# Gathers of embedding rows over 128 partitions in place of 125 in a graph layer with pre-normalisation

## The chip, the cores and the metric

The kernel runs on one core of one Trainium2 chip. The metric is the device time of the whole program in microseconds (us); lower is better. The median of three runs of the kernel before is 3028.99 us (3013.37 to 3032.68).

## The reference, cut to what matters

There are 12,500 nodes of 256 features and 212,500 edges of 128 features. Each node's row gets a projected sum over its outgoing edges, two gates, and one row out of each of two tables of 512 rows, chosen by its in-degree and its out-degree.

```python
in_deg  = minimum(segment_sum(ones, dst), 511)
out_deg = minimum(segment_sum(ones, src), 511)
sum3d   = segment_sum(edge_attr @ W_sum + b_sum, src)
cent    = sigmoid(centralities @ W_cent + b_cent)
vor     = sigmoid(voronoi_values @ W_vor + b_vor)
h   = relu(layernorm(x))
out = x + (h + z_in[in_deg] + z_out[out_deg] + cent + vor + sum3d)
```

## The kernel before, in words

Nodes are cut into 100 windows of 125 (`NODE_P`): node p*100+w is row p of window w, so a window stands on 125 of the 128 partitions. There are 128 partitions in every SBUF tile, and partitions 125 to 127 of a window's rows are never used for output.

**The sort.** 1,660 tiles of 128 edges and a rest of 20 go through a loop over 416 groups of four (q). VectorE (DVE) makes one-hot matrices, TensorE (PE) ranks the edges by window with them, ScalarE (ACT) reads the positions out, and GpSimd (POOL) writes each tile's 128 rows of 520 bytes to their places in HBM with an indirect DMA (L513; L517 for the last 20). Edges are sorted in four segments. Beside this, in places that the table `side` sets, the same engines load sorted rows back and sum them, count in-degrees into `deg_i` (L708, one column per window, 125 partitions), and work out normalisation and gates into `base`. This takes the time up to about 2716 us. `base` holds 55 windows at a time, so 45 of them ("guests") are stored to the output array and are loaded back in the tail (L464).

**The tail.** From about 2716 us the last segment's pieces are loaded (130 KB each, L408, on SP's queue, 12 slots) and folded into `acc` (L670 on DVE, four matmuls L1001, L697 on DVE). There are 250 pieces; after the first 150 (`ahead`), one window's sums are finished by each further piece. From there the loop makes one step per window, 100 in all, and each step holds: the piece; the fold L697; `out_i`, the out-degrees of two windows in one instruction every second step (L767); the transpose of the sums (L1010 on PE), its copy (L878 on ACT), the bias (L927 on ACT), the product with `w_sum` (L1019 on PE) and three adds on DVE into the window's row of `base`: product (L780), z_in row and z_out row (both L785). Five windows make one store (L886, ACT's queue, 560 KB and 65 KB), and the guests' rows come back from step 28 on, five windows at a time.

**The gathers.** POOL has nothing else in the tail. Its list `z_order` has 200 indirect DMAs, all at L530: 100 of z_in (indices in `deg_i`) and 100 of z_out (indices in `out_i`), each bringing the 125 table rows (1,024 bytes each) of one window into a place. z_out of a window waits for that window's `out_i` (`s_out_deg`). The places are two rings. Ring "others" has 15 places in `edge_ring` and serves all z_out and the first 55 z_in; ring "guests" has 18 places laid over `dst_parts`, `key_f` and `gate_normed`, which the tail no longer needs, and serves the 45 z_in of the guests. A gather into a place waits until the add of the gather that had it before is done (`s_added`). The add (L785) reads partitions 0 to 124 alone. In the step count, `out_i` of a pair of windows is made 5 and 6 steps ahead of the adds that need the rows (`COUNT_LAG` 3, `Z_LAG` 9).

Before the first z_out there are 69 gathers of z_in in the list (51 for the first 55 windows, 18 for guests). The 131 left are 100 of z_out and 31 of z_in.

## Time and profile before

| | us |
|---|---|
| runs, median of 3 | 3028.99 |
| runs, lowest and highest | 3013.37, 3032.68 |
| profiled execution, span | 3079.2 |
| POOL busy in the profiled execution | 1853.9 (60%) |
| DVE busy | 1683.0 (55%) |
| PE busy | 1621.7 (53%) |
| ACT busy | 819.8 (27%) |

The profiled execution is known by its span alone; no time around it was recorded beside it. It is another execution than the three runs. Engines overlap, so their busy times do not add up to the span, and DVE instructions overlap by a part of their length too. "Idle before" is what an engine waited ahead of the instructions of a group, with the instruction or transfer that ended it. A transfer's time in the chain of waits runs from its issue to its landing.

### The profile page before, as it was taken

What the parts mean: (1) busy time and instruction counts of PE and PEld (TensorE: products, weight loads), DVE (VectorE), ACT (ScalarE), POOL (GpSimd) and SP (SyncE); (2) the same over time, 40 slices, a digit from 0 to 9 for tenths busy, and PEclk for the clock granted to TensorE, in tenths of its full rate; (3) what the DMA queues carried; (4) which work ended last, traced back from release to release, by engine and by line L of the source; (5) the groups of instructions that cost most, each with busy time, mean ns of one, the idle gap of its engine ahead of it and who ended that gap; (6) DMA issues with size and microseconds to landing.
All of it is one profiled execution on the core that took longest, in us unless ns stands there. A gap on an engine that the chain in (4) does not pass through costs nothing.

```text
span 3079.2 us, 40112 instructions
## 1 busy us (share of the span) xinstructions
PE 1621.7 (53%) x8689; PEld 1230.9 (40%) x8689; DVE 1683.0 (55%) x5737; ACT 819.8 (27%) x4073; POOL 1853.9 (60%) x1869
## 2 busy tenths in 40 slices
PE   5644555455555432226555554444456665568766
PEld 1223444344333320014444444333355554456655
DVE  7554456666666631346656654333455554468866
ACT  3312222232322332442232322222222222200323
POOL 5556665556565667665555655656655555556676
PEclk7756666666666655557767777767777777789988
DMA  4245433334444443334555555555556666579896
GB/s 122 85 127 151 116 106 107 99 104 122 122 121 121 126 135 106 88 107 137 155 152 164 160 160 161 143 151 148 155 156 181 183 187 178 169 189 231 210 248 187
DMA packets 485070, 451.89 MB, mean 147 GB/s; under 512 B 72407, under 2 KB 444637, under 8 KB 484828
## 3 DMA queue, kind: packets, MB, share of 16 engines
q1 hardware_dynamic: 402782, 300.08, 37.0%
q0 software_dynamic: 78752, 136.44, 14.1%
q10 hardware_dynamic: 3294, 12.80, 1.3%
q8 instruction: 71, 1.16, 0.2%
q14 instruction: 171, 1.40, 0.2%
HBM read 319.28 MB, written 129.59 MB: 146 GB/s over the span
## 4 chain that ended last, share of the span: by engine, by line
another core or an unknown queue 34%; DVE 19%; PE 17%; issue 15%; ACT 7%; DMA 3%; SPq 2%; POOL 2%; DVEq 1%; ACTq 0%; POOLq 0%
PE bank L1001 8%; ACT junk L864 6%; DVE hot_dh L605 3%; DVE hot_n L670 3%; DVE acc L697 2%; DVE hot_dl L605 2%; PE bank L949 2%; POOL sorted L513 2%; DMA edge_ring<-in_L_gnn_z_out_dram,out_i 2%; SPq L408 2%; DVE gate_normed L736 2%; PE bank L984 1%; PE bank L1026 1%; DVE hot_t L605 1%
## 5 line engine op out<-in xcount | busy, mean ns | idle before, releaser
L513 POOL DMA_INDIRECT sorted<-edge_ring,pos_i x1660 | 1605.8, 967 | 1103.1 <-DVE pos_i L799 633.4
L1001 PE MATMUL bank<-piece_ring,hot_n 128*125 128x129 f32 x4920 | 885.4, 336 | 260.0 <-DVE hot_n L670 209.0
L864 ACT ACTIVATE junk<-bank,mark_col 128x100 bf16<-128x100 f32 x1664 | 550.4, 343 | 1748.6 <-remote 1221.3
L1001 PEld LDWEIGHTS bank<-piece_ring,hot_n 128*125 128x125 f32 x4920 | 823.2, 241 | 367.0 <-DVE hot_n L670 248.7
L697 DVE TENSOR_TENSOR acc<-bank,acc 125x129 f32 x1230 | 352.8, 287 | 698.6 <-remote 523.9
L984 PE MATMUL bank<-hot_w,after_b 128*128 128x400 bf16 x416 | 189.3, 455 | 806.1 <-ACT junk L864 560.7
L670 DVE SCALAR_TENSOR_TENSOR hot_n<-bank,wkey,piece_ring 128x250 f32<-128x250 f32 x1230 | 579.9, 472 | 11.8 <-issue 5.2
L984 PEld LDWEIGHTS bank<-hot_w,after_b 128*128 128x128 bf16 x416 | 49.5, 119 | 866.8 <-ACT junk L864 594.3
L864 ACT ACTIVATION_READ_ACCUMULATOR junk<-bank,mark_col 128x1 f32 x1664 | 338.1, 203 | 12.3 <-issue 12.3
L605 DVE TENSOR_TENSOR hot_dl<-dst_parts,bank 128x400 bf16<-128x400 bf16 x416 | 148.0, 356 | 337.1 <-remote 305.5
L1026 PE MATMUL bank<-hot_dl,hot_dh 128*125 128x100 bf16 x1661 | 207.2, 276 | 237.4 <-DVE hot_dh L605 197.6
L1026 PEld LDWEIGHTS bank<-hot_dl,hot_dh 128*125 128x125 bf16 x1661 | 182.1, 188 | 268.7 <-DVE hot_dh L605 213.8
L949 PE MATMUL bank<-hot_t,ones_b 128*128 128x400 bf16 x416 | 157.1, 430 | 84.5 <-DVE hot_t L605 52.9
L985 PE MATMUL bank<-hot_w,unmark_b 128*128 128x400 bf16 x416 | 191.1, 459 | 0.0
L978 PE MATMUL bank<-hot_w,before_b 128*128 128x400 bf16 x416 | 189.4, 455 | 0.2 <-DVE hot_w L605 0.2
L605 DVE TENSOR_TENSOR hot_dh<-dst_parts,bank 128x500 bf16<-128x500 bf16 x416 | 170.7, 410 | 0.0
L605 DVE TENSOR_TENSOR hot_t<-src_w,bank 128x400 bf16<-128x400 bf16 x416 | 136.7, 358 | 36.3 <-PE bank L949 22.4
L530 POOL DMA_INDIRECT edge_ring<-in_L_gnn_z_out_dram,out_i x100 | 123.6, 1236 | 53.6 <-DVE out_i L767 18.4
L605 DVE TENSOR_TENSOR hot_w<-src_w,bank 128x400 bf16<-128x400 bf16 x416 | 148.2, 357 | 0.1
L799 DVE CAST pos_i<-pos_f 128x4 int32<-128x4 f32 x416 | 75.0, 180 | 115.7 <-remote 57.5
L949 PEld LDWEIGHTS bank<-hot_t,ones_b 128*128 128x128 bf16 x416 | 47.6, 114 | 176.4 <-DVE hot_t L605 93.2
L927 ACT ACTIVATE bank<-rows_b,acc 125x256 f32<-125x256 f32 x100 | 47.8, 478 | 241.4 <-DVE acc L697 159.2
(109 smaller groups left out, 1183.2 us busy)
## 6 DMA issues: line engine op xcount, KB each, us to landing
piece_ring<-sorted SPq DMA_DIRECT2D x1230, 130.0 KB
edge_ring<-in_edge_attr_dram SPq DMA_DIRECT2D x332, 320.0 KB
sorted<-edge_ring,pos_i POOLq DMA_INDIRECT x1660
base<-in_x_dram SPq DMA_DIRECT2D x20, 560.0 KB
out_dram<-base ACTq DMA_DIRECT2D x19, 560.0 KB
out_dram<-base SPq DMA_DIRECT2D x9, 560.0 KB
base<-out_dram SPq DMA_DIRECT2D x9, 560.0 KB
edge_ring<-in_L_gnn_z_out_dram,out_i POOLq DMA_INDIRECT x100
```

What stands on the lines that cost most here:

```text
L513: g.indirect_dma_start(rows, bass.IndirectOffsetOnAxis(index, 0), edge_ring[:, slot, at, :], None).then_inc(s_scatter[slot], 16)
L530: g.indirect_dma_start(places[n % len(places)][0:NODE_P, :], None, table[:, :], bass.IndirectOffsetOnAxis(index[0:NODE_P, w:w + 1], 0)).th ...
L605: return v.tensor_tensor(to, part.unsqueeze(2).to_broadcast([P, 2, n, 2]), iota_pair[:, 0:n, :].unsqueeze(1).to_broadcast([P, 2, n, 2]), A ...
L670: v.scalar_tensor_tensor(out=hot_n[:, n % HOT_SLOTS, 0:G, :], in0=iota_ps.unsqueeze(1).to_broadcast([P, G, LOC]), scalar=wkey[:, s % 2, c: ...
L697: v.tensor_tensor(to, piece_sums(s, c), to, ALU.add).then_inc(s_summed, 1)
L864: last = a.activation(junk[:, t, :], part[:, t // 2, :, t % 2], ACT.Relu, bias=mark_col[:, :], accum_out=pos_f[:, q % 4, t:t + 1])
L949: return t_.matmul(ps_total[:, 0:SW * QUAD], ones_b[:, :], hot.rearrange("p g w t -> p (g w t)"), start=(h == quad0[s]), stop=(h == quad0[ ...
L978: t_.matmul(ps_rank, before_b[:, :], hot, start=False, stop=True, skip_group_check=True).then_inc(s_rank, 1)
L984: t_.matmul(ps_rank, after_b[:, :], hot, start=False, stop=False, skip_group_check=True)
L985: t_.matmul(ps_rank, unmark_b[:, :], hot, start=False, stop=True, skip_group_check=True).then_inc(s_based, 1)
L1001: last = t_.matmul(to, hot_n[:, n % HOT_SLOTS, k, :], piece_ring[:, n % PIECE_SLOTS, k, 0:SUM], start=(k == 0), stop=(k == ROW_GROUPS[s] - 1))
L1026: last = t_.matmul(ps_in_count, hot_dh[:, b, t // 2, :, t % 2], hot_dl[:, b, t // 2, :, t % 2], start=(h == 0 and t == 0), stop=(h == NQ - ...
```

## The change

The indirect DMA of L530 covers all 128 partitions of its place and of its index column. `deg_i` and `out_i` are written on partitions 0 to 124 only, so both are cleared whole at the start; partitions 125 to 127 then hold index 0 and get row 0 of the table, which no instruction reads.

```diff
@@ gpsimd: gathers
-                g.indirect_dma_start(places[n % len(places)][0:NODE_P, :], None, table[:, :],
-                                     bass.IndirectOffsetOnAxis(index[0:NODE_P, w:w + 1], 0)
+                g.indirect_dma_start(places[n % len(places)][:, :], None, table[:, :],
+                                     bass.IndirectOffsetOnAxis(index[:, w:w + 1], 0)
                                      ).then_inc(landed[n % len(places)], 16)
@@ vector: clears at the start
             v.memset(mark_col[:, :], -MARK)
             v.memset(zero_col[:, :], 0.0)
+            v.memset(deg_i[:, :], 0)
+            v.memset(out_i[:, :], 0)
             v.memset(ones_b[:, :], 1.0).then_inc(s_cleared, 1)
```

On POOL, in the tail, the order of the gathers before (the names are the place's tile, the table in HBM and the index table):

```order
21 L530 DMA edge_ring<-in_L_gnn_z_out_dram,out_i 125x256 x2
22 L530 DMA edge_ring<-in_L_gnn_z_in_dram,deg_i 125x256
23 L530 DMA edge_ring<-in_L_gnn_z_out_dram,out_i 125x256 x3
24 L530 DMA edge_ring<-in_L_gnn_z_in_dram,deg_i 125x256
25 L530 DMA edge_ring<-in_L_gnn_z_out_dram,out_i 125x256 x3
```

The same place of the changed kernel:

```order
21 L530 DMA edge_ring<-in_L_gnn_z_out_dram,out_i 128x256 x2
22 L530 DMA edge_ring<-in_L_gnn_z_in_dram,deg_i 128x256
23 L530 DMA edge_ring<-in_L_gnn_z_out_dram,out_i 128x256 x3
24 L530 DMA edge_ring<-in_L_gnn_z_in_dram,deg_i 128x256
25 L530 DMA edge_ring<-in_L_gnn_z_out_dram,out_i 128x256 x3
```

No gather moves in the list; each has three more partitions. On DVE, at the very start, the changed kernel has:

```order
9 L558 MEMSET mark_col 128x1
10 L559 MEMSET zero_col 128x1
11 L560 MEMSET deg_i 128x100
12 L561 MEMSET out_i 128x100
13 L562 MEMSET ones_b 128x128
14 L563 MEMSET ones_f 128x1
```

Rows 11 and 12 are new, ahead of the clear of `ones_b`, which raises `s_cleared`; all later lines of the program stand two lines further down.

## Rows read from the trace of the kernel before

**Rows 1.** The page: span, and busy time by engine.
```profile
span 3079.2 us, 40112 instructions
PE 1621.7 (53%) x8689; PEld 1230.9 (40%) x8689; DVE 1683.0 (55%) x5737; ACT 819.8 (27%) x4073; POOL 1853.9 (60%) x1869
```

**Rows 2.** Chain of waits, 2860 to 3046 us: start, length, what.
```profile
by line: DMA edge_ring<-in_L_gnn_z_out_dram,out_i 31.8%; issue 19.3%; PE bank L1019 14.5%; PE bank L1001 10.5%; PE bank L1010 6.7%; DVE base L785 2.3%; DVE base L780 2.1%; DVE hot_n L670 2.1%; DVE acc L697 1.8%; DVEq L385 1.6%; POOL edge_ri
...
2903.20 9.83 DMA edge_ring<-in_L_gnn_z_out_dram,out_i
...
2948.12 13.03 DMA edge_ring<-in_L_gnn_z_out_dram,out_i
```

**Rows 3.** Windows of the tail: stretch, busy time (instructions), clock, DMA share, GB/s.
```profile
core 0: us, PE busy (x) PEld busy (x) DVE busy (x) ACT busy (x) POOL busy (x), PEclk, DMA share, GB/s
2860.00:2890.00 30.00, 20.81 (x119) 17.46 (x119) 20.97 (x69) 9.81 (x28) 23.74 (x20) 0.94 0.64 168
2890.00:2918.00 28.00, 21.89 (x129) 17.75 (x128) 22.96 (x78) 10.57 (x31) 18.34 (x16) 1.00 1.00 255
2918.00:3046.00 128.00, 91.74 (x440) 74.70 (x438) 86.38 (x281) 38.33 (x109) 101.96 (x83) 0.85 0.96 232
3046.00:3062.00 16.00, 12.82 (x77) 10.78 (x78) 13.48 (x46) 6.66 (x19) 11.42 (x10) 1.00 0.58 160
```

**Rows 4.** Windows for L780 alone, one instruction per step.
```profile
2890.00:2918.00 28.00, 6.47 (x16) 1.00 1.00 255
2918.00:3046.00 128.00, 23.26 (x55) 0.85 0.96 232
3046.00:3062.00 16.00, 3.84 (x9) 1.00 0.58 160
```

**Rows 5.** Groups of POOL, 2918 to 3046 us: busy, mean ns, idle before.
```profile
L530 POOL DMA_INDIRECT edge_ring<-in_L_gnn_z_out_dram,out_i x56 | 69.6, 1244 | 18.3 <-issue 11.9 <-DVE base L785 3.9 <-DVE out_i L767 1.3
L530 POOL DMA_INDIRECT dst_parts<-in_L_gnn_z_in_dram,deg_i x12 | 14.6, 1216 | 3.7 <-issue 3.4 <-DVE base L780 0.3
L530 POOL DMA_INDIRECT key_f<-in_L_gnn_z_in_dram,deg_i x9 | 11.0, 1225 | 2.8 <-issue 1.8 <-DVE base L785 0.6 <-DVE base L780 0.3
L530 POOL DMA_INDIRECT gate_normed<-in_L_gnn_z_in_dram,deg_i x6 | 7.5, 1248 | 1.8 <-issue 1.5 <-DVE base L785 0.3
```

**Rows 6.** Group of DVE, 2918 to 3046 us, that adds rows from edge_ring.
```profile
L785 DVE TENSOR_TENSOR base<-edge_ring,base 125x256 f32<-125x256 f32 x55 | 23.2, 422 | 34.7 <-DMA edge_ring<-in_L_gnn_z_out_dram,out_i 18.2 <-issue 14.9 <-DVE base L780 0.8
```

**Rows 7.** POOL in order of time: start, length, [idle before].
```profile
2860.45 1.20 POOL L530 DMA_INDIRECT edge_ring<-in_L_gnn_z_out_dram,out_i  x1 [14.93 <-DVE out_i L767]
2861.96 1.20 POOL L530 DMA_INDIRECT edge_ring<-in_L_gnn_z_out_dram,out_i  x1 [0.31 <-DVE out_i L767]
...
2913.99 1.20 POOL L530 DMA_INDIRECT edge_ring<-in_L_gnn_z_out_dram,out_i  x1 [2.51 <-DVE base L780]
...
3046.99 1.44 POOL L530 DMA_INDIRECT edge_ring<-in_L_gnn_z_out_dram,out_i  x1 [0.94 <-DVE out_i L767]
```

**Rows 8.** Groups of POOL over the whole span: scatters and the gathers of z_out.
```profile
L513 POOL DMA_INDIRECT sorted<-edge_ring,pos_i x1660 | 1605.8, 967 | 1103.1 <-DVE pos_i L799 633.4 <-issue 469.1 <-ACT edge_ring L871 0.6
L530 POOL DMA_INDIRECT edge_ring<-in_L_gnn_z_out_dram,out_i x100 | 123.6, 1236 | 53.6 <-DVE out_i L767 18.4 <-issue 17.7 <-DVE base L780 10.6
...
L517 POOL DMA_INDIRECT sorted<-edge_last,pos_i x1 | 0.9, 897 | 0.3 <-issue 0.3
```

**Rows 9.** DMA queues, 2200 to 2300 us: packets, MB, share of 16 engines.
```profile
q0 software_dynamic: 1857, 3.87, 10.9%
```

**Rows 10.** POOL's instructions in two windows: 2200 to 2300, 2716 to 2860.
```profile
2200.00:2300.00 100.00, 56.05 (x60) 0.74 0.54 151
2716.00:2860.00 144.00, 83.16 (x69) 0.93 0.89 226
```

**Rows 11.** DMA queues, 2716 to 2860 us.
```profile
q0 software_dynamic: 8832, 8.91, 24.2%
```

**Rows 12.** Start of the program on DVE, in order of time.
```profile
1.36 0.17 DVE L560 MEMSET ones_b<- 128x128 bf16 x1
...
5.93 0.21 DVE L583 TENSOR_SCALAR base<-base 128x100 f32<-128x100 int32 x1 [1.43 <-DMA base<-in_src_dram]
```

## The prediction

> **What bounds the kernel now.** I read the page's busy times first [rows 1]: no engine is over 60%, so shares say nothing and the stage that the change touches has to be read by itself. All 200 gathers lie after 2716 us. The first 69 are z_in rows of windows that wait for nothing else, gathered while DVE works on pieces. So the chain of waits comes next, for 2860 to 3046 us [rows 2]. Its largest part, 31.8%, is "DMA edge_ring<-z_out": from the issue of a gather to its landing, 9.83 us at 2903 and 13.03 us at 2948. That looks like a slow transfer. The windows view and POOL's own groups tell it otherwise for most of the stretch.
>
> In 2918 to 3046 us POOL has 83 gathers [rows 3, 5]. They are busy for 69.6+14.6+11.0+7.5 = 102.7 us and idle for 18.3+3.7+2.8+1.8 = 26.6 us, together 129 of 128 us, and 26.6/83 = 0.32 us is the gap that stands even between two gathers issued back to back (0.31 at 2861.96 [rows 7]). POOL never rests there: one gather takes 1.24+0.32 = 1.55 us, and a step that needs 83/55 = 1.51 gathers [rows 4] takes 128/55 = 2.33 us. The reader should see that POOL's issue sets this pace. DVE shows the other side: before the adds from `edge_ring` it is idle for 34.7 us in 55 steps, 18.2 of it ended by a z_out landing, and 14.9 by "issue", which is a release whose source the profile doesn't show [rows 6]. Other waits of DVE in the stretch are small against this.
>
> Two stretches beside it are different. In 2890 to 2918 us there are 16 gathers for 16 steps, and POOL waits (2.51 us at 2913.99 [rows 7]), because it has caught up with the indices that DVE makes. A step takes 28/16 = 1.75 us. In 3046 to 3062 us it is 16/9 = 1.78 us, with POOL waiting again. This is the pace of the loop through DVE, PE and ACT when gathers don't hold it. From 3062 on, the last steps run through PE alone.
>
> **The change, part by part.**
>
> (a) *POOL's time per gather.* 125 rows take 1.236 us [rows 8]. No row shows a gather of 128 partitions, so I bound it by neighbours: a scatter of 128 partitions takes 0.967 us and one of 20 takes 0.897 us [rows 8], so the number of rows costs almost nothing (0.07 us for 108 rows, 0.6 ns each) and 105 rows more than 20 don't explain 1.236. Something else does. The queue rows name it: 60 scatters made 1857 packets, about 31 each [rows 9, 10], but 69 gathers made 8832, exactly 128 each [rows 10, 11]. A scatter's 67 KB in some 31 packets are 16 of 4.2 KB (eight rows of 520 bytes) and as many small ones, so each of 16 engines moves eight rows and signals. At that size a gather's 125 KB would need 32 and 16, 48 in all. One split that does give 128 is that 125 = 5 x 25 goes to five engines only, with 25 rows each in seven packets plus a signal, and that the other eleven queues get as many small fillers: 8 x 16. 128 rows = 16 x 8 can be split as the scatter's are. I take the scatter's figure, 0.97 us, as the same count of partitions in the same kind of instruction; the other end is no gain at all, 1.24 us, if a gather is simply dearer than a scatter. Saving 0.27 us per gather.
>
> The Trainium skill, "DMA: Bandwidth & Descriptors", section "Why a DMA increments its semaphore by 16 and not by 1", says that the engines used are the largest number up to 16 that divides the slowest dimension. By that rule 125 gives 5 and 128 gives 16; the 128 packets agree. The same section has an exception that speaks against the change: software-generated direct copies may use all 16 engines with an uneven share. By the exception the old gather would already be spread and the sum would be zero; 128 packets in place of some 48 do not fit it.
>
> (b) *The stretch 2918 to 3046 us.* POOL's need falls from 128 to 83 x (0.97+0.32) = 107 us, 21 us less. What is late next? The loop's own pace, 55 x 1.77 = 97 us, would allow 31. DMA is the nearer limit: 232 GB/s x 128 us = 29.7 MB, and at 255 GB/s, the most that these windows show [rows 3], that is 116 us, which allows 12 us only. DMA share is 0.96 already. But the fillers go (80 packets of each gather), and one engine need no longer move 25 rows while eleven move none, so I expect more than 255. Ends: 0 (POOL doesn't get faster) and 31. I take 17, between DMA's 12 and POOL's 21.
>
> (c) *The stretch 2890 to 2918 us.* POOL waits for indices, DVE hardly for rows. A shorter landing helps a few adds. Ends 0 and 4; I take 2.
>
> (d) *2860 to 2890 us.* POOL is back to back here (20 gathers, 30 us) but is ahead: the first z_out add comes some five steps after its index. Ends 0 and 20 x 0.27 = 5; I take 1.
>
> (e) *The first 69 gathers and the end.* In 2716 to 2860 us POOL is busy for 83 of 144 us [rows 10] and waits for places that DVE frees; faster issue is hidden behind DVE's pieces. After 3062 us only five gathers are left. Both 0.
>
> (f) *Bytes.* 200 x 3 x 1,024 bytes = 0.6 MB more; the 83 gathers of (b) have 0.25 MB, 1 us at 255 GB/s, charged there. All three spare partitions read row 0.
>
> (g) *The two clears.* They stand ahead of `s_cleared` on DVE. `ones_b`, 128 columns, took 0.17 us [rows 12], so two of 100 columns cost at most 0.34 us. The signal releases ACT's small index load, for which DVE then waits 1.43 us, so this is on the path, in full: 0.3 us. No other engine's work is queued behind them.
>
> Sum: 17+2+1-1-0.3 = 19 us, rounded. It is made against the profiled span of 3079.2 us, which gives 3060. That execution is 50 us longer than the median of the runs; none of the terms comes from that difference, so I take the 19 us off the median: 3028.99 - 19 = 3010 us.
>
> **The rivals.**
>
> *R1: no gain, because a gather costs POOL what it costs.* For it: every gather in the trace takes at least 1.2 us whatever its table and place, and its rows are twice as long as a scatter's. Against it: row count alone costs 0.6 ns, and the packets show a different split. The landing might still shorten, but POOL would hold the pace: 0 to 3 us, 3028 us.
>
> *R2: the full release.* If DMA isn't a limit once its load is even, the tail falls to the loop's pace: 31 in (b), 4 in (c), 3 in (d), less 1: 37 us, 2992 us. For it: DVE's 34.7 us of waiting before these adds is about that size. Against it: POOL's 107 us would still stand over 97, unless its mean falls under the scatter's.
>
> *R3: contention.* A gather now has to be served by all 16 engines, each of which also has 5 KB packets of stores and guests' rows, and lands with the slowest of them. The place is steps 28 to 73, where DMA share is about 1. If each landing there took 13.03 us where it takes 9.83 now, a loop over the five steps between index and add gets 3.2 us longer. 45 steps have nine such loops: +29 us, and with POOL's gain lost in waiting, 3059 us with the 1 us for bytes. It decides as soon as index to landing is over five steps of 2.33 us = 11.7 us. Against it: an engine serves two packets of a gather in place of seven, so it should be done sooner.
>
> *R4: the change doesn't do what it says*: the cleared partitions make no difference in the split. Same time as R1, and counted there.
>
> **How the numbers follow.** The forecast (POOL at about 0.97 us, 10 to 30 us gained) has 0.66, R1 0.14, R2 0.14, R3 0.06. The predicted time is the forecast's, 3010 us. Gains of 30 and 10 us are 2999 and 3019. The range takes in R1 and a good part of the way to R2: 2991 to 3031. A measurement of this kernel tells about 1%, 30 us, from no change. Faster by over that is R2 and the edge of the forecast, 0.19. Slower by over that is half of R3 and a little for what I haven't thought of, 0.04. The rest is 0.77.
>
> **What would show it.** POOL's gathers at L530 near 0.97 us in place of 1.236, and 48 packets each in place of 128; in the middle of the tail, POOL no longer back to back; the 34.7 us before the adds from `edge_ring` down to some 10; steps of 2.0 us in place of 2.33; landings in the chain of 5 us or less in place of 9 to 13. DMA share near 1 with over 255 GB/s would say that DMA is the next limit. Gathers that still take 1.2 us make (a) wrong and with it nearly all. Gathers of 0.97 us with a tail that isn't shorter make (b) wrong.

## The result, and the profile of the changed kernel

The changed kernel took **3061.68 us** (median of 4 runs, 3052.53 to 3066.99) against 3027.90 us (4 runs, 3013.37 to 3032.68) of the kernel before beside it: ratio **1.0113**, 95% interval 1.0084 to 1.0143, some 34 us slower. The forecast was 3010 us in a range of 2991 to 3031. The experiments below add a second finding that turns the first one round: on three other chips the same change makes the kernel 1.7% *faster*.

The page of the changed kernel, for [rows 1] the span and busy times, then the row of the DMA queue that carries scatters and gathers, and the chain that ended last by engine:

```profile
span 3065.2 us, 40114 instructions
PE 1626.2 (53%) x8689; PEld 1235.1 (40%) x8689; DVE 1676.7 (55%) x5739; ACT 819.8 (27%) x4073; POOL 1806.1 (59%) x1869
...
q0 software_dynamic: 62752, 136.83, 13.4%
...
another core or an unknown queue 37%; DVE 21%; PE 16%; issue 13%; ACT 7%; POOL 3%; DVEq 2%; DMA 1%; SPq 0%; ACTq 0%; POOLq 0%
```

POOL's busy time fell by 48 us. The queue carried 78752 packets in a profile of the kernel before (its row is shown with e13 below) and carries 62752 now: 16000 fewer, 80 for each of 200 gathers, so 128 have become 48.

The profiled execution of the kernel before (3079.2 us) is no good yardstick for the total: its last scatter was issued at 2712 us, against 2668 to 2674 us in e1 to e4 and the changed kernel. It looks like the runs on chip B below (3073 us), but its chip is not on record. From here on stages are compared, and the yardstick is the kernel before run again (e1_same, span 3026.5 us).

POOL's gathers and DVE's adds of the changed kernel. First two groups of POOL over the whole span, which answer to [rows 8], then three groups of DVE in 2902 to 3030 us, which answer to [rows 6]; columns as there (busy, mean ns, idle before and what ended it):

```profile
L530 POOL DMA_INDIRECT edge_ring<-in_L_gnn_z_out_dram,out_i x100 | 104.0, 1040 | 101.5 <-DVE out_i L769 73.6 <-issue 17.8 <-DVE base L782 5.5
L530 POOL DMA_INDIRECT edge_ring<-in_L_gnn_z_in_dram,deg_i x55 | 52.0, 945 | 68.7 <-DVE base L787 60.3 <-issue 8.5
```

```profile
L787 DVE TENSOR_TENSOR base<-edge_ring,base 125x256 f32<-125x256 f32 x53 | 22.1, 418 | 0.3 <-DMA edge_ring<-in_L_gnn_z_out_dram,out_i 0.3
L782 DVE TENSOR_TENSOR base<-bank,base 125x256 f32<-125x256 f32 x53 | 22.1, 417 | 12.2 <-remote 8.3 <-PE bank L1021 1.9 <-issue 1.6
L699 DVE TENSOR_TENSOR acc<-bank,acc 125x129 f32 x53 | 15.0, 283 | 32.4 <-remote 20.1 <-PE bank L1003 11.6 <-issue 0.6
```

What the prediction wanted of the gathers came true in the main. They are shorter: z_in rows take 945 ns in place of 1202, z_out rows 1040 on the mean in place of 1236 (their median is 949, the longest took 1355). And the add from `edge_ring`, which stood idle for 34.7 us in such a stretch [rows 6], now waits for 0.3 us. POOL is no longer back to back: it waits 73.6 us for the indices that DVE makes, 18.4 before [rows 8]. But the time didn't go away. It turned up at DVE's adds of matmul results, at L699 and L782, as waits for "remote". That word stands where a wait ended and the profile shows no engine or transfer that was still at work on what was waited for. L699 waits for no other engine than TensorE; L782 waits for TensorE's product and, from window 55 on, for the guests' rows too.

The windows of the tail, which answer to [rows 3] (stretch, busy time and instructions, clock, DMA share, GB/s):

```profile
2874.00:2902.00 28.00, 23.04 (x142) 19.44 (x141) 25.12 (x86) 12.43 (x36) 17.67 (x17) 1.00 0.91 282
2902.00:3030.00 128.00, 85.52 (x422) 73.61 (x422) 83.11 (x273) 36.82 (x104) 79.95 (x81) 0.81 0.76 227
```

In the 128 us in the middle every engine did less than before, POOL 80.0 us in place of 102.0 (its gathers are shorter), PE 85.5 in place of 91.7, DVE 83.1 in place of 86.4, and the DMA share fell from 0.96 to 0.76. No engine is full and no queue is. What holds the loop has no row of its own.

It shows best ahead of that, where 21 gathers follow each other without a gap and nothing else changes. First what was waited for (total, times, longest) in 2786 to 2820 us, then the windows around it:

```profile
DVE acc L699 <- remote: 21.3, 5, 6.0
```

```profile
2776.00:2786.00 10.00, 8.66 (x57) 7.06 (x56) 9.81 (x34) 0.00 (x0) 4.11 (x5) 1.00 0.85 255
2786.00:2796.00 10.00, 5.23 (x33) 4.18 (x34) 5.50 (x17) 0.00 (x0) 7.56 (x9) 0.88 0.68 205
2796.00:2806.00 10.00, 2.22 (x8) 1.61 (x8) 1.12 (x4) 0.00 (x0) 7.57 (x9) 0.50 0.46 132
2806.00:2816.00 10.00, 2.44 (x8) 1.85 (x8) 1.25 (x4) 0.00 (x0) 5.41 (x6) 0.50 0.40 118
2816.00:2826.00 10.00, 8.04 (x47) 7.33 (x48) 9.02 (x30) 0.00 (x0) 0.00 (x0) 0.76 0.53 151
```

DVE's column (the third) goes 9.81, 5.50, 1.12, 1.25, 9.02: for 20 us it does next to nothing, PE with it, and both are back within 4 us of the end of POOL's last gather there (2812.9 us). In order of time, two rows of PE and three of DVE (start, length, idle before):

```profile
2790.76 0.71 PE L1003 MATMUL bank<-piece_ring,hot_n 128*125 128x129 f32 x4 [0.68 <-issue]
...
2795.77 1.22 PE L1003 MATMUL bank<-piece_ring,hot_n 128*125 128x129 f32 x4 [2.53 <-DVE hot_n L672]
```

```profile
2790.24 0.47 DVE L672 SCALAR_TENSOR_TENSOR hot_n<-bank,wkey,piece_ring 128x250 f32<-128x250 f32 x1
...
2799.95 0.29 DVE L699 TENSOR_TENSOR acc<-bank,acc 125x129 f32 x1 [4.24 <-remote]
...
2805.55 0.29 DVE L699 TENSOR_TENSOR acc<-bank,acc 125x129 f32 x1 [4.92 <-remote]
```

In this segment DVE's add L699 runs two pieces behind L672 (`FOLD_LAG` 2). The add at 2799.95 us therefore belongs to the piece that L672 prepared at 2790.24, and whose four matmuls ended at 2790.76 + 0.71 = 2791.47 us. The add came 8.5 us later, and for the last 4.2 us of them DVE was idle. The piece of the matmuls that ended at 2796.99 was added at 2812.55, 15.6 us later.

What is late is the signal. An engine tells the others that an instruction is done by raising a semaphore, and the trace holds the times at which semaphores were raised. TensorE's semaphore for the piece that ended at 2791.47 was raised at 2799.82, and DVE and SP's loads, which both wait for it, went on at that moment. The next two came at 2805.42 and 2812.42, 12.2 and 15.4 us after their matmuls; the three after them came together, at 2816.67 to 2816.79, when the gathers had stopped. DVE's own signals came within 0.1 us in the same stretch. The clock isn't the trigger: it was full when the first of these matmuls ran (0.71 us for four) and fell to 0.50 only when PE stood idle between them. The ends of matmuls are modelled in the profile, but the same is seen below with an instruction of ACT.

The same had been in the profile of the kernel before, in the sort, where POOL issues scatters without a gap; I hadn't read it. Its chain by engine, and ACT's group that waits for PE's counts:

```profile
another core or an unknown queue 34%; DVE 19%; PE 17%; issue 15%; ACT 7%; DMA 3%; SPq 2%; POOL 2%; DVEq 1%; ACTq 0%; POOLq 0%
...
L864 ACT ACTIVATE junk<-bank,mark_col 128x100 bf16<-128x100 f32 x1664 | 550.4, 343 | 1748.6 <-remote 1221.3
```

In the sort it is not TensorE alone. One of its stretches, with ACT's last read of a group, DVE's conversion and PE's matmul that wait for it:

```profile
1216.36 0.20 ACT L864 ACTIVATION_READ_ACCUMULATOR junk<-bank,mark_col 128x1 f32 x1 [1.61 <-issue]
```

```profile
1224.10 0.39 DVE L799 CAST pos_i<-pos_f 128x4 int32<-128x4 f32 x1 [10.90 <-remote]
```

```profile
1224.12 0.52 PE L984 MATMUL bank<-hot_w,after_b 128*128 128x400 bf16 x1 [10.73 <-remote]
```

ACT was done at 1216.56 us, its semaphore was raised at 1224.07, 7.5 us later, and PE and DVE started together. So signals of ACT come late too.

**The theory of the pace**, which the experiments test: when POOL issues indirect DMAs of 128 rows back to back, one each 1.25 us, the signals that TensorE's results are there (below: late results) come late by microseconds. Gathers of 125 rows came each 1.50 us and did it much less. Rivals: the clears or the moved start; the 128 rows themselves (their spread over all 16 engines) whatever the pace.

### The profile page after: what moved, and what is told of

The parts are those of the page before. It is cut to its first block, busy times and chain, and to the rows that moved or that the text cites. A ratio compares the mean times of both kernels' runs of the same rounds, so it can differ in the third digit from the quotient of the medians.

```text
span 3065.2 us, 40114 instructions
## 1 busy us (share of the span) xinstructions
PE 1626.2 (53%) x8689; PEld 1235.1 (40%) x8689; DVE 1676.7 (55%) x5739; ACT 819.8 (27%) x4073; POOL 1806.1 (59%) x1869
## 3 DMA queue, kind: packets, MB, share of 16 engines
q0 software_dynamic: 62752, 136.83, 13.4%
## 4 chain that ended last, share of the span: by engine, by line
another core or an unknown queue 37%; DVE 21%; PE 16%; issue 13%; ACT 7%; POOL 3%; DVEq 2%; DMA 1%; SPq 0%; ACTq 0%; POOLq 0%
PE bank L1003 7%; ACT junk L866 6%; POOL sorted L513 3%; DVE hot_n L672 3%; DVE acc L699 3%; DVE hot_dh L607 3%; PE bank L951 3%; DVE hot_dl L607 2%; DVE gate_normed L738 2%; PE bank L1021 2%; DVE hot_t L607 1%; PE bank L986 1%; DVE hot_w L607 1%; PE bank L980 1%
## 5 line engine op out<-in xcount | busy, mean ns | idle before, releaser
L699 DVE TENSOR_TENSOR acc<-bank,acc 125x129 f32 x1230 | 348.3, 283 | 731.0 <-remote 530.3
L672 DVE SCALAR_TENSOR_TENSOR hot_n<-bank,wkey,piece_ring 128x250 f32<-128x250 f32 x1230 | 575.2, 468 | 5.9 <-issue 4.3
L607 DVE TENSOR_TENSOR hot_dl<-dst_parts,bank 128x400 bf16<-128x400 bf16 x416 | 146.0, 351 | 325.7 <-remote 281.1
L530 POOL DMA_INDIRECT edge_ring<-in_L_gnn_z_out_dram,out_i x100 | 104.0, 1040 | 101.5 <-DVE out_i L769 73.6
L1021 PE MATMUL bank<-w_sb,hot_t 128*125 128x256 f32 x200 | 78.9, 481 | 64.4 <-ACT hot_t L880 41.8
```

The lines of the kernel that those rows point to most:

```text
L607: return v.tensor_tensor(to, part.unsqueeze(2).to_broadcast([P, 2, n, 2]), iota_pair[:, 0:n, :].unsqueeze(1).to_broadcast([P, 2, n, 2]), A ...
L672: v.scalar_tensor_tensor(out=hot_n[:, n % HOT_SLOTS, 0:G, :], in0=iota_ps.unsqueeze(1).to_broadcast([P, G, LOC]), scalar=wkey[:, s % 2, c: ...
L699: v.tensor_tensor(to, piece_sums(s, c), to, ALU.add).then_inc(s_summed, 1)
L1021: t_.matmul(ps_y[n % 2][0:NODE_P, 0:D], sumT[:, n % 2, :], w_sb[:, :], start=False, stop=True, skip_group_check=True).then_inc(s_y, 1)
```

## The experiments

They fell on five chips. By the time of the kernel before these are of two kinds, and this turned out to matter more than any edit:

| runs | chip | kernel before, us |
|---|---|---|
| e1 to e4 | A | 3028.03 |
| e5 to e8 | B | 3073.45 |
| e9 to e12 | C | 2479.83 |
| e13 to e16 | D | 2479.36 |
| e17, e18 | E | 2482.66 |

All ratios are against the kernel before on the same chip. ("Theory A" and "theory B" in the expectations of e1 to e4 have nothing to do with the chips' letters.) In the diffs the declarations of semaphores and counters are left out. The stages of each profile, from the starts of POOL's first gather and first z_out gather, and the span:

| profile (chip) | first gather, us | to first z_out gather | from there to the end | both |
|---|---|---|---|---|
| before (not on record) | 2716.7 | 143.8 | 218.8 | 362.5 |
| e1, before (A) | 2674.2 | 137.9 | 214.4 | 352.3 |
| e2, before with the clears (A) | 2673.1 | 135.0 | 210.4 | 345.5 |
| changed kernel (its chip is like A) | 2676.7 | 169.4 | 219.1 | 388.5 |
| e4, changed (A) | 2670.9 | 166.7 | 224.8 | 391.5 |
| e3, changed, clears on POOL (A) | 2674.4 | 163.2 | 224.2 | 387.4 |
| e8, sort paced, gathers of 125 rows (B) | 2602.8 | 146.0 | 219.7 | 365.7 |
| e5, each 1.49 us (B) | 2706.6 | 149.1 | 213.7 | 362.9 |
| e6, each 1.65 us (B) | 2714.9 | 129.1 | 228.4 | 357.5 |
| e7, 1.25 us but spread (B) | 2705.2 | 149.1 | 228.3 | 377.4 |
| e13, before (D) | 2136.7 | 129.8 | 211.0 | 340.8 |
| e14, changed (D) | 2140.2 | 114.3 | 181.6 | 296.0 |
| e15, each 1.49 us (D) | 2140.8 | 114.5 | 209.4 | 323.9 |
| e16, first 69 of 125 rows (D) | 2138.5 | 128.0 | 187.1 | 315.1 |
| e17, first 69 each 1.49 us (E) | 2142.0 | 113.9 | 183.2 | 297.1 |
| e18, changed (E) | 2140.6 | 114.0 | 183.7 | 297.7 |

**e1_same** is the kernel before, unchanged.

> The kernel before, unchanged, for a second profile of it: what two profiles of one kernel differ by, and what two timings of it differ by. Both theories expect a ratio of 1.000 within 0.4%. If its profile puts the first gather within 10 us of 2716.7 us and the time from there to the end within 5 us of 362.5 us, the two profiles of before and after can be compared stage by stage; if it is off by 30 us or more, the sort's length is chance from one execution to the next and the stages have to be compared over several profiles.

Measured: 3027.15 us, 1.0002 (0.9982 to 1.0023). Its first gather came 42 us earlier than in the profile of the kernel before, so by the expectation stages have to be compared over several profiles; three with gathers of 125 rows on this kind of chip (before, e1, e2) differ by 9 us in the first stage and by 8 in the second. At the place in the program where the changed kernel's DVE falls to 1.12 us in 10, its windows are

```profile
2773.00:2783.00 10.00, 8.02 (x51) 6.24 (x49) 8.70 (x29) 0.00 (x0) 7.86 (x8) 1.00 1.08 249
2783.00:2793.00 10.00, 7.75 (x39) 6.14 (x40) 7.55 (x25) 0.00 (x0) 7.93 (x7) 0.86 0.99 228
```

DVE goes on at 8.70 and 7.55 us in 10, with POOL as busy as there but with 7 or 8 gathers in place of 9.

**e2_clears** has the two clears alone:

```diff
+            v.memset(deg_i[:, :], 0)
+            v.memset(out_i[:, :], 0)
```

> The kernel before with the two clears alone, gathers of 125 rows. Theory A (the loss lies in the tail, where a gather now needs all 16 DMA engines): ratio 1.000, since the start is 0.5 us later at most. Theory B (the loss comes from the start: the first keys are later by 0.5 us, or the program is placed otherwise, and the sort runs longer): ratio 1.011, with the tail as before.

Measured: 3025.98 us, 1.0009 (0.9986 to 1.0033). The clears, and what they delay at the start, cost nothing that can be measured.

**e3_gather** has the gathers of 128 rows, with the clears made by POOL in place of DVE:

```diff
+            g.memset(deg_i[:, :], 0)
+            g.memset(out_i[:, :], 0)
-            v.memset(deg_i[:, :], 0)
-            v.memset(out_i[:, :], 0)
```

> Gathers of 128 rows, with the two clears on POOL ahead of its last iota in place of DVE. Theory A: ratio 1.011, first gather to end 20 to 30 us longer than before, and first keys at 5.9 us as before. Theory B: ratio 1.000 or less.

Measured: 3064.98 us, 1.0135 (1.0093 to 1.0178), as theory A had it. With the clears off DVE the cost stays, and e2 had the clears without it: the cost is in the gathers.

**e4_again** is the changed kernel once more.

> The changed kernel again, for a second profile: ratio 1.011 by both theories. Theory A expects first gather to end near 388.5 us again and POOL's gathers at 0.95 us; by theory B that length varies and the sort is longer than before's on the mean.

Measured: 3055.09 us, 1.0097 (1.0066 to 1.0128). The cost is there again.

**e5_pace** keeps the 128 rows and slows POOL down: an iota of 128 columns behind each gather, for which POOL waits, so that gathers come each 1.49 us.

```diff
+                g.iota(start_of[:, 0, 0:128], pattern=[[1, 128]], base=0, channel_multiplier=0,
+                       allow_small_or_imprecise_dtypes=True).then_inc(s_pad, 1)
+                pads += 1
+                pool.wait_ge(s_pad, pads)
```

> The changed kernel with a small iota of POOL (128 columns) behind each gather, and a wait for it, so that gathers come every 1.5 to 1.6 us as before the change, not every 1.25 us. Theory P (what costs time is the pace: while POOL issues DMAs of 128 rows back to back, PE's results come late): first gather to first fold back from 34 us to some 22 us, first z_in add to first z_out gather back from 131 us to some 114 us, ratio to before 1.000 or slightly less. Theory Q (what costs time is that each gather uses all 16 DMA engines, at any pace): both stretches stay at some 34 and 131 us, ratio 1.011 or more.

Measured on chip B: 3076.93 us, 1.0006 (0.9988 to 1.0025). **e6_wider** has an iota of 320 columns there, one gather each 1.65 us.

> As the last, with an iota of 320 columns: a gather every 1.9 us or so. Theory P: no late PE results in the two early stretches (22 and 114 us or less), but the steps from 28 to 75 need 1.5 gathers each and now wait for POOL: 2.9 us per step, some 25 us more, ratio 1.008. Theory Q: 34 and 131 us and the slower steps as well, ratio 1.02.

Measured: 3068.26 us, 0.9978 (0.9957 to 0.9999). **e7_spread** isn't paced (1.25 us), but mixes the guests into the first 69 gathers and ties each of them to a fold, so that no run of them is long (the new order of the list is left out here):

```diff
+                if at < len(early) and 2 * at > 14:
+                    pool.wait_ge(s_summed, piece0[NS - 1] + 2 * at - 14)
```

> The changed kernel with the first 69 gathers spread out: the 18 of guests are mixed into the 51 others, and gather n (from the eighth on) waits until 2n-14 pieces of the last segment are folded, so that no run of back-to-back gathers is left before the first z_out. The pace of the later gathers is untouched. Theory P: the two early stretches fall to 22 and 114 us or less, the steps 28 to 75 stay 9 us longer than before, ratio 1.002. Theory Q: each of the 69 gathers costs what it cost, stretches together still 29 us longer than before, ratio 1.011.

Measured: 3086.42 us, 1.0042 (1.0025 to 1.0059). Of the totals, e5's fits theory P (1.000) and not Q (1.011), e7's lies between P's 1.002 and Q's 1.011 and nearer to P, and e6's is below both (1.008 and 1.02). P's 136 us for the first stage (22 + 114) were missed: e5 and e7 took 149.1. They had been taken from chip A; e8 below, on chip B with gathers of 125 rows, took 146.0. The traces tell more. Waits of DVE's fold for remote between the first gather and the first z_out gather (total, times, longest) were, in the order changed kernel, e3, e4, then e1, e5 and e7:

```profile
DVE acc L699 <- remote: 32.8, 6, 11.6
```

```profile
DVE acc L699 <- remote: 30.0, 6, 9.2
```

```profile
DVE acc L699 <- remote: 32.1, 6, 7.4
```

```profile
DVE acc L697 <- remote: 1.2, 1, 1.2
```

```profile
DVE acc L705 <- remote: 1.7, 1, 1.7
```

```profile
DVE acc L706 <- remote: 6.1, 1, 6.1
```

and e6 has none. So 30 to 33 us wherever gathers of 128 rows run on at 1.25 us, 1 to 2 us at 1.5 us whether they have 125 rows or 128 (3.5 in the kernel before's own profile, 1.5 in e8), none at 1.65, and 6 where the runs are broken up. Behind the first z_out gather, ACT waits for PE's sums at its copy (`copy_sum`); the rows are of the changed kernel, of e1, of e5 and of e7:

```profile
ACT hot_t L880 <- remote: 52.5, 16, 5.1
```

```profile
ACT hot_t L878 <- remote: 3.5, 2, 2.0
```

```profile
ACT hot_t L886 <- remote: 18.5, 9, 2.6
```

```profile
ACT hot_t L887 <- remote: 62.3, 18, 8.0
```

e6 again has none. There the order is the same, 1.25, 1.25 (e7), 1.49, 1.50, 1.65 us with 52.5, 62.3, 18.5, 3.5 and 0 us. That goes by pace and not by rows: e5 to e7 all have 128. That e5 has more than e1 at nearly one pace is the chip for the most part: e8, on e5's chip and with gathers of 125 rows each 1.50 us, has 15.8.

The raised semaphores say the same. From the first gather on, TensorE's signals that came over 1 us after the last instruction that could have raised them add up, on chip A, to 57 and 66 us with 125 rows (e2, e1) and to 216 to 262 us with 128 rows at 1.25 us (e3, e4, changed kernel); on chip B to 119 us with 125 rows (e8), 147 at 1.49 us (e5), 224 in e7 and 37 at 1.65 us (e6). The last is three signals, and three, of 28 to 34 us in all, stand in the traces of chips C to E as well (e9, e11 to e15, e18).

The tail of e8 is also the yardstick that e5 to e7 lack, since it was not touched there. Against its 365.7 us, e5 took 2.8 us less, e6 8.2 less and e7 11.7 more; the whole kernels took 3.5 more, 5.2 less and 13.0 more than the kernel before on that chip. So on one chip 128 rows at 1.49 us cost next to nothing, and at 1.25 us, even in short runs, some 12 us. One thing limits this: no run of the changed kernel itself stood on chip B.

**e8_sortpace** asks whether the same holds where the kernel spends most of its time. It is the kernel before, with a waited iota of 32 columns ahead of each scatter of the sort, which then come each 1.45 us in place of 1.26:

```diff
+                    g.iota(pad[:, :], pattern=[[1, 32]], base=0, channel_multiplier=0,
+                           allow_small_or_imprecise_dtypes=True).then_inc(s_pad, 1)
+                    pool.wait_ge(s_pad, c + 1)
```

> The kernel before with a small iota of POOL and a wait ahead of each of the 1660 scatters of the sort, so that they come every 1.4 to 1.5 us and not every 1.26 us. Gathers as before. Theory P applied to the sort: ACT and DVE wait there for PE results that are late while scatters run back to back (ACT's largest wait in the profile of before, 1221 us, has no visible source), so the sort gets shorter by a per cent or more. Theory Q says nothing of the sort; if POOL's own work is what the sort waits for, it gets longer, by up to 1660 x 0.2 = 330 us.

Measured on chip B: 2963.25 us, **0.9626** (0.9596 to 0.9656). 1660 extra instructions and waits on POOL make the kernel 110 us faster. POOL's scatters and the iotas in its trace:

```profile
L518 POOL DMA_INDIRECT sorted<-edge_ring,pos_i x1660 | 1639.0, 987 | 488.6 <-issue 345.5 <-POOL pad L511 142.3 <-ACT edge_ring L876 0.8
L511 POOL IOTA pad<- 128x32 f32 x1661 | 286.7, 173 | 181.3 <-DVE pos_i L804 141.4 <-issue 4.7
```

In the kernel before, POOL had waited 633.4 us at this line for `pos_i`, the product of the loop over PE, ACT and DVE [rows 8]. The paced kernel waits for it 141.4 us, at the iota. Late signals got fewer, but most are left: against e5, whose sort is not paced, on the same chip, ACT's waits for remote at the ranks are 1190.9 us in place of 1306.3, DVE's at the histogram 99.4 in place of 275.8, and PE's for ACT's positions, 131.2 before, are gone. TensorE's late signals of the sort add up to 4234 us in place of 5540. That the pause made the kernel faster is measured; that it did so by the wider pace and not by the wait that it puts ahead of each scatter was to be told by e11, and wasn't.

The next four runs were to build on that, and showed that it isn't a property of the kernel. **e12_again**, the changed kernel:

> The changed kernel once more, on the chip of this batch, as the yardstick of e9 and e10 and for the question whether its cost hangs on the chip: 1.010 of the kernel before, 1.007 to 1.014, if the change costs the same on every chip. If it is within 0.003 of the kernel before, the paced gathers of e5_pace and e6_wider (1.001 and 0.998 on another chip) had shown nothing.

Measured on chip C: 2439.70 us, **0.9834** (0.9820 to 0.9847), against 2479.83 us of the kernel before. Both of the expected outcomes are missed: the change is not as slow as on chip A, and not level either, but 40 us faster, and the kernel before is 18% faster than on A. **e9_sortpace_128** (e8's pacing and the change):

> The sort paced as in e8_sortpace (a waited iota of 32 columns ahead of each scatter), and the change with it (gathers of 128 partitions, not paced, each about 1.25 us, and the two clears). Theory of the pace: the two do not overlap in time, so the cost of the change stands beside the gain of the sort: against the kernel before 0.962 + 0.011 = 0.973, 0.970 to 0.977; in the trace the last z_out gathers' DVE waits are gone, first gather to first fold is 30 us or more (before 23) and first z_in add to first z_out gather about 130 us (e8_sortpace: 122). Rival (the cost of the change is a remainder of the sort's own delay, which a faster sort takes away): 0.962, 0.959 to 0.966.

Measured: 2764.00 us, 1.1151 (1.1136 to 1.1166). **e10_both_paced** (with e5's pacing too):

> As e9_sortpace_128, and each gather followed by a waited iota of 128 columns as in e5_pace, so that gathers come each 1.49 us. Theory of the pace: the cost of the change is gone and a little of its use is left: 0.962, 0.959 to 0.965 against the kernel before, and 0.008 to 0.013 below e9_sortpace_128; first z_in add to first z_out gather about 120 us. Rival (the gathers' pace does not matter once the sort is faster, the iotas only add POOL time): level with e9_sortpace_128 within 0.003.

Measured: 2792.38 us, 1.1263 (1.1247 to 1.1278). **e11_sort_wider** (the kernel before, two waited iotas ahead of each scatter, which come each 1.68 us for the most part):

```diff
+                    for twice in range(2):
+                        g.iota(pad[:, :], pattern=[[1, 32]], base=0, channel_multiplier=0,
+                               allow_small_or_imprecise_dtypes=True).then_inc(s_pad, 1)
+                        pool.wait_ge(s_pad, 2 * c + 1 + twice)
```

> The kernel before with two waited iotas of 32 columns ahead of each scatter, so that scatters come each 1.65 us or so in place of 1.45 in e8_sortpace and 1.26 before; gathers as before. Theory of the pace: what is left of the late results falls further (the ACT wait for remote in the sort well under the 1190.9 us of e8_sortpace), but 1660 scatters by 1.65 us are 2740 us on POOL alone if they cannot be hidden, longer than the 2570 us that the sort takes in e8_sortpace, so the time is 1.02 to 1.06 of the kernel before, with POOL the bound and few remote waits. Rival (the gain of e8_sortpace is not of the pace but of the wait that stands ahead of each scatter, which lets the queue run empty): the remote wait stays near 1190 us although the pace is wider.

Measured: 3278.73 us, 1.3220 (1.3200 to 1.3240). All three expectations fell, for one reason: nothing in the traces of chip C waits for remote, not even in e12, whose scatters come each 1.26 us as on A. The pacing that gained 3.7% on B costs 324 us here (e9 against e12), which is 1660 scatters by 0.19 us, 315 us, nearly in full: POOL is the bound of the sort. The chains by engine of e12 and of e11 say so:

```profile
POOL 50%; issue 19%; DMA 13%; DVE 9%; PE 6%; ACT 1%; SPq 1%; DVEq 1%; ACTq 0%; POOLq 0%
```

```profile
POOL 68%; issue 22%; DMA 6%; PE 2%; DVE 2%; DVEq 0%; SPq 0%; POOLq 0%; ACT 0%; ACTq 0%
```

"Another core or an unknown queue" is in neither, where it had 34 to 37% on the slower chips. e9 to e11 therefore say nothing on late results; they only price POOL's time.

Where the change gains on such a chip is told by the next six. **e13_before** and **e14_after**, on chip D:

> The kernel before, unchanged: 1.000, 0.998 to 1.002. Its trace is the yardstick of e14 to e16 on this chip. If the chip is of the kind of e12 (about 2480 us), the trace shows hardly any wait for remote, scatters each 1.26 us without a pause, and z_out gathers that come each 1.50 us as the bound of the last 100 us. If it is of the kind of e1 (about 3030 us), some 150 pauses of over 2 us in the scatters, as in e1_same.

> The changed kernel beside e13_before. Theory: its sign hangs on whether results of the tensor engine come late on the chip. On a chip of about 2480 us: 0.983, 0.981 to 0.986, the 40 us gained ahead of the last z_out gathers, 100 us x 2 of gathers that come each 1.25 us in place of 1.50 being 50 us at most. On a chip of about 3030 us: 1.011, 1.008 to 1.014. Rival (the gain on the chip of e12 was chance of that chip's kernel before): 1.00 on a fast chip.

Measured: 2480.58 us, 1.0008 (0.9999 to 1.0017), and 2438.03 us, **0.9834** (0.9820 to 0.9847). Both are as expected. The stages of the table fell by 129.8 - 114.3 = 15.5 and 211.0 - 181.6 = 29.4 us. Windows of e14 at the place of the 21 gathers in a row, to be held against those of the changed kernel above:

```profile
2218.00:2228.00 10.00, 8.87 (x59) 7.41 (x59) 9.63 (x33) 0.00 (x0) 7.56 (x9) 1.00 0.93 274
2228.00:2238.00 10.00, 8.51 (x56) 6.79 (x54) 9.81 (x33) 0.00 (x0) 7.56 (x9) 1.00 0.95 288
```

The same program, the same nine gathers in 10 us, 7.56 us of POOL in both; but DVE is busy for 9.63 and 9.81 us in place of 5.50 and 1.12. A back-to-back run of gathers is harmless on this chip. The instructions themselves are no faster there: a scatter takes 966 ns (968 in e1), the fold 284 (285), ACT's read of a bank 340 (343).

**e15_pace** is e5's kernel, and **e16_late_128** gathers 125 rows in the first 69 and 128 in the other 131 (`at` counts the gathers):

```diff
+                many = P if at >= 69 else NODE_P
-                g.indirect_dma_start(places[n % len(places)][:, :], None, table[:, :],
-                                     bass.IndirectOffsetOnAxis(index[:, w:w + 1], 0)
+                g.indirect_dma_start(places[n % len(places)][0:many, :], None, table[:, :],
+                                     bass.IndirectOffsetOnAxis(index[0:many, w:w + 1], 0)
```

> The changed kernel with its gathers held to one each 1.49 us by a waited iota of 128 columns (the same kernel as e5_pace), beside e14_after. On a chip of about 3030 us: 1.001, 0.999 to 1.003 by the theory of the pace, level with e14_after (1.011) by its rival, that 128 rows cost whatever their pace. On a chip of about 2480 us: the gain is undone, 0.998 to 1.008 of the kernel before, since gathers come as slowly as before.

> The changed kernel with gathers of 125 rows for the first 69 of the 200 (those ahead of the first z_out), 128 rows for the other 131. On a chip of about 3030 us the theory of the pace puts 29 of the 38 us into the first 69: 1.003, 1.000 to 1.006. Rival (the steps after the first z_out cost it): 1.008 to 1.011. On a chip of about 2480 us: if the gain comes from the gathers after the first z_out, all of it is kept, 0.983 to 0.987; if it comes from the first 69, 0.995 to 1.0.

Measured: 2465.81 us, 0.9944 (0.9931 to 0.9958), and 2450.81 us, 0.9885 (0.9870 to 0.9900). Both missed what was expected on such a chip (0.998 to 1.008 for e15; 0.983 to 0.987 or 0.995 to 1.0 for e16), because there are two gains and not one. e15 keeps the first (114.5 us to the first z_out gather) and loses nearly all of the second (209.4 us); e16 loses the first (128.0) and keeps most of the second (187.1). Windows from the first add of z_in rows to the first z_out gather and from there to the end, of e13, e14 and e15:

```profile
2144.00:2267.00 123.00, 100.56 (x610) 81.80 (x610) 108.61 (x352) 0.55 (x2) 77.47 (x65) 0.96 1.08 239
2267.00:2478.00 211.00, 158.07 (x777) 128.09 (x776) 148.16 (x490) 68.95 (x199) 159.39 (x131) 0.86 0.91 223
```

```profile
2146.00:2255.00 109.00, 95.56 (x611) 78.91 (x610) 106.34 (x354) 0.48 (x1) 61.83 (x66) 0.99 0.91 273
2255.00:2436.00 181.00, 139.22 (x779) 114.12 (x777) 145.89 (x490) 68.80 (x199) 131.77 (x131) 0.96 0.86 262
```

```profile
2147.00:2255.00 108.00, 95.32 (x608) 78.61 (x607) 105.95 (x354) 0.48 (x1) 79.75 (x130) 0.99 0.92 274
2255.00:2465.00 210.00, 154.12 (x781) 126.55 (x779) 149.15 (x491) 69.28 (x199) 161.90 (x262) 0.87 0.76 226
```

In the first stretch it is the DMA engines: their share is 1.08 at 239 GB/s with gathers of 125 rows and 0.91 at 273 GB/s with 128, at either pace, and DVE goes from 108.6 busy in 123 us to 106.3 in 109, that is, full. It had waited 10.6 us, 19 times, for pieces that came late, and now 0.7 us, once. In the second it is POOL's issue: 131 gathers take 159.4 us and 131 gaps of 0.3 us, 199 of 211 us, and now 131.8 + 39 = 171 of 181. The landings got shorter too, a median of 7.7 us in e13 and 4.2 us in e14:

```profile
DMA to landing us min/median/max: 3.8/7.7/13.8
```

```profile
DMA to landing us min/median/max: 2.8/4.2/8.6
```

and in e13 the queue carried as many packets as in the first profile of the kernel before:

```profile
q0 software_dynamic: 78752, 136.44, 17.6%
```

**e17_first_paced** paces the first 69 gathers (1.49 us) and not the others, beside **e18_after**, on chip E:

> The changed kernel with a waited iota of 128 columns behind each of its first 69 gathers (one each 1.49 us there), none behind the other 131 (each 1.25 us). On a chip of about 2480 us: e15_pace and e14_after took 108.1 and 108.5 us from the first z_in add to the first z_out gather, so the pace is free there and all of the gain is kept: 0.983, 0.981 to 0.986, level with e18_after. On a chip of about 3030 us: the cost of the first 69 is gone and that of the others stays, 1.003, 0.998 to 1.006; by the rival (128 rows cost there whatever their pace) level with e18_after at 1.010.

> The changed kernel, the yardstick of e17_first_paced: 0.983, 0.981 to 0.986, on a chip of about 2480 us; 1.011, 1.008 to 1.014, on one of about 3030 us.

Measured: 2440.91 us, 0.9832 (0.9817 to 0.9846), and 2440.15 us, 0.9827 (0.9814 to 0.9841). As expected: the pace of the first 69 is free on such a chip, which settles that the first gain comes from how the rows are moved and not from POOL's time. Fewer packets and the even spread over the engines change together in every run, so which of the two it is stays open. What e17 does on a chip of the other kind was not measured; it is the version I would try first there, since it takes away the 21 gathers that follow each other at 1.25 us, and those at the start. The 131 others, which took some 8 us more there, would stay.

## Why the prediction was wrong

**The step that failed** is (e), "faster issue is hidden behind DVE's pieces ... Both 0". It looked only at whether faster gathers could help. On the chips of its kind they hurt: the stretch from first gather to first z_out gather took 163.2, 166.7 and 169.4 us with 128 rows, and 135.0, 137.9 and 143.8 with 125, so 28 us more on the mean. DVE waited there 30 to 33 us for late results of TensorE, in place of 1 to 4. Step (b) failed with it: it took 17 us off what comes behind, and from the first z_out gather to the end it was 222.7 us on the mean in place of 214.5, 8 us more. Together that is 36 us (40 without the first profile of the kernel before, which may be another chip's), against the 34 us of the result. The prediction had given 0.04 to a time that is slower by over 30 us.

(a) was right in its mechanism and to the packet, and the row count is no cost. Its size was a little off: 0.27 us per gather was to be saved, and over all 200 gathers the mean fell from 1.22 to 0.99 us, 0.23. (It is 0.945 in place of 1.20 where nothing disturbs them, but z_out's mean is 1.04 and not 0.97.) The sizes of the packets bear the split out. In the tail before the change there are six packets of 4096 bytes to one of 1024 (1280 and 210 in 2716 to 2805 us), which is 25 rows on each of five engines, four rows a packet, and one left over; most of the others have 16 bytes. After it there are two of 4096 bytes to one of 4 (1472 and 736 in 2676 to 2785 us), 32 and 16 per gather. The Trainium skill, "DMA: Bandwidth & Descriptors", section "Why a DMA increments its semaphore by 16 and not by 1", gives 5 engines for 125 and 16 for 128 by its rule; the packets agree, and its exception, uneven use of all 16 by software-generated copies, doesn't show in these gathers.

(b), 17 us in the middle of the tail, was right about what POOL would do and wrong about what comes next. POOL did stop being the bound and the adds did stop waiting for rows (0.3 us). On the chip of the result the loop's own pace, which I took at 1.77 us from a stretch of 28 us, didn't hold while gathers ran at 1.25 us: a step took 128/53 = 2.42 us in place of 2.33. On chip D (b) to (d) together, 20 us by the prediction, gained 29.4: the limit of "255 GB/s, the most that these windows show" was none, since from the first z_out gather on e14 has 262 GB/s over 181 us at a DMA share of 0.86, and its windows ahead of that up to 288.

(c) and (d) can't be told apart from (b) in the result. (e) on chips C to E was mis-sized too, 0 for 15.5 us. There the cover failed to be one: POOL's idle time there was indeed free (e17), but DMA's wasn't, and the DMA share of 0.89 there [rows 10] had been the warning. (g) was right: nothing measurable (e2). (f), 1 us, is too small to be told apart in any run.

Of the rivals, R3 had named the time (3059 us) and the wrong reason. A landing with the slowest of 16 engines was to cost; the add waited for hardly any (0.3 us), and where the traces have landings they got shorter (7.7 to 4.2 us, chip D). R1 and R4 fell with the packets. R2, the full release at -37 us, is what chips C, D and E did, -40 to -43 us, though only 29 of it in R2's place.

The cause under all of this was in the page of the kernel before, and no step read it: a chain with 34% "another core or an unknown queue" and 1221.3 us of ACT's waits for remote. A third of that chain was waits that no row explained, and the change altered how tightly POOL issues.

**What stays open.** Why the signals of TensorE, and in the sort of ACT, come late: no row shows it. It isn't the load of the DMA engines (share 0.40 to 0.46 while it was worst), nor the program, which is the same on all chips. The mean granted clock of the kernel before is 0.70 on A and B and 0.76 to 0.77 on C to E, but e11, on C, has 0.69 and no wait for remote, so it goes with the idle time and doesn't make the lateness. What the two kinds of chips differ in isn't shown. One more difference is in the traces: those of A and B have lost many of their records of raised semaphores (e1 has 5703 of the 9451 that PE, ACT and DVE raise), those of C to E next to none (e13 has 9438). Whether the losses and the lateness have one source, and whether profiling has a part in it, no run tells. That pace is the trigger rests on the waits in traces of A and B, on e5 to e7 beside the tail of e8, and in part on e8's gain, not on the changed kernel beside them on one chip. The chip of the result itself is put with A by its time (3028 us) and by its waits.

## What to carry to other kernels

Before you put a price on a change, account for the largest share of the chain that ended last, even where the profile has no name for it; a term of "nothing, it is hidden" needs a look at each resource that the faster step will press on, not only at the engine that it relieves. Measure on more than one chip when waits for "remote" are in the trace: the same change gave +1.1% and -1.7%, and pacing the sort -3.7% and +13%. In this kernel an indirect gather of 128 partitions in place of 125 cost POOL 0.25 us less and the DMA engines 80 packets fewer, and it paid where POOL's issue and the DMA engines were the bound (chips C to E).

## What the runs showed of the hardware

- Gathers of 125 rows of 1 KB make 128 packets and hold POOL for 1.20 us, of 128 rows 48 packets and 0.945 us where nothing disturbs them; one follows another in 1.50 and 1.25 us.
- On two chips of five, and on that of the result, TensorE's signals reached DVE, ACT and SP late while POOL issued indirect DMAs back to back at 1.25 us: by 8.5 and 15.6 us in the rows read, in waits of up to 11.6 us in the tail. In the sort ACT's signals did so too (7.5 us in the rows shown), and a forced pause of 0.19 us ahead of each scatter made the kernel 110 us faster there (e8). With a gather each 1.65 us (e6) no wait for remote was left in the tail.
- On the three other chips the kernel before took 2480 us in place of 3028 or 3073, with no such wait in any trace, though the instructions take as long (e1, e13).
- On chip D, with the gathers spread over all engines, the DMA engines moved 273 GB/s at a share of 0.91 where they had moved 239 at 1.08 (e13, e14).
